# Two preactivated 5x5 self-correlation layers on one core: where the next unit's group average stands in TensorE's order

## What is computed

```python
norm = jnp.sqrt(jnp.sum(feature * feature, axis=1, keepdims=True))
fn = feature / jnp.maximum(norm, EPS)
fp = jnp.pad(fn, ((0, 0), (0, 0), (PAD, PAD), (PAD, PAD)))
corr = jnp.stack([jnp.sum(fp[:, :, r:h + r, cc:w + cc] * fn, axis=1)
                  for cc in range(K) for r in range(K)], axis=1)
cat = jnp.concatenate([feature, corr], axis=1)          # 512 + 25 channels
y = jnp.einsum('oc,bchw->bohw', conv_w, cat) + conv_b[None, :, None, None]
return jax.nn.relu(y)
```

## Time and profile before

| what | value |
|---|---|
| median of three runs | 527.68 us (525.36 to 530.27) |
| profiled execution, its own time | 526.55 us |
| span of the profiled execution | 524.8 us |
| TensorE busy | 470.0 us (90%) |
| VectorE busy | 370.0 us (71%) |
| ScalarE busy | 276.4 us (53%) |
| GpSimd busy | 127.6 us (24%) |
| mean granted TensorE clock | 0.967 of full speed |

### The profile page before, as it was taken

How to read it: one execution, slowest core, us unless ns; L and a number is a source line. 1 busy time by engine, 2 the same in 40 slices (tenths; PEclk the granted TensorE clock), 3 DMA queues, 4 the chain that set the end, 5 groups by cost and what they waited for, 6 DMA issues and landing times.

```text
span 524.8 us, 9885 instructions
## 1 busy us (share of the span) xinstructions
PE 470.0 (90%) x3880; PEld 259.5 (49%) x3880; DVE 370.0 (71%) x868; ACT 276.4 (53%) x370; POOL 127.6 (24%) x179
## 2 busy tenths in 40 slices
PE   0557597679996999999998999999999999999996
PEld 0443445364643646464553646464646455464442
DVE  4788896768967687786869495868878695623322
ACT  1443455447383665839383755657493848433222
POOL 3534420131330313131220313131312212140400
PEclk9978898879998999999999999999999999999999
DMA  8271263542220465447566673232322325463432
GB/s 297 108 252 51 87 201 117 138 117 54 82 82 8 118 213 164 128 158 242 203 213 223 208 267 117 55 115 55 86 85 50 114 72 176 146 189 106 148 115 107
DMA packets 50876, 71.76 MB, mean 137 GB/s; under 512 B 12276, under 2 KB 37932, under 8 KB 50830
## 3 DMA queue, kind: packets, MB, share of 16 engines
q1 hardware_dynamic: 41038, 62.21, 35.5%
q0 software_dynamic: 9792, 8.92, 7.1%
HBM read 34.97 MB, written 33.59 MB: 131 GB/s over the span
## 4 chain that ended last, share of the span: by engine, by line
PE 60%; DVE 18%; ACT 7%; DMA 6%; issue 4%; POOL 3%; SPq 1%; DVEq 0%; ACTq 0%; POOLq 0%
PE conv_ps L567 42%; PE gram_ps L487 8%; DVE operands L837 4%; DVE stats L790 4%; PE conv_ps L576 4%; DMA vol<-corr_h 4%; ACT operands L661 3%; ACT v L667 3%; PE gram_ps L499 2%; DVE xs L920 2%; POOL v L430 2%; DVE operands L843 1%; DMA xs<-in_x_dram 1%; PE turn_ps L557 1%; POOL vol L293 1%
## 5 line engine op out<-in xcount | busy, mean ns | idle before, releaser
L567 PE MATMUL conv_ps<-operands,wh 128*128 128x512 f16 x1024 | 326.0, 383 | 0.3 <-DVE wl L908 0.3
L567 PE MATMUL conv_ps<-operands,wl 128*128 128x512 f16 x512 | 195.8, 382 | 0.0
L694 ACT ACTIVATE act_out<-conv_ps,bias,wdown 128x512 f32<-128x512 f32 x128 | 95.9, 772 | 133.9 <-PE conv_ps L576 125.1
L567 PEld LDWEIGHTS conv_ps<-operands,wh 128*128 128x128 f16 x1024 | 100.8, 98 | 122.4 <-issue 4.8
L837 DVE TENSOR_TENSOR operands<-v,operands 128x1024 f16<-128x1024 f32 x64 | 81.5, 1274 | 59.1 <-ACT v L667 53.9
L920 DVE TENSOR_TENSOR xs<-xs,act_out 128x512 f32<-128x512 f32 x128 | 85.9, 683 | 36.6 <-ACT act_out L694 36.3
L790 DVE BATCH_NORM_STATS2 stats<-xs 128x6 f32<-128x512 f32 x128 | 79.7, 678 | 5.5 <-DMA xs<-in_x_dram 5.5
L661 ACT ACTIVATE operands<-xs,affine 128x1024 f16<-128x1024 f32 x64 | 78.5, 1233 | 5.6 <-DVE affine L830 5.6
L567 PEld LDWEIGHTS conv_ps<-operands,wl 128*128 128x128 f16 x512 | 50.5, 99 | 57.9 <-issue 1.5
L487 PE MATMUL gram_ps<-operands 128*64 128x192 f16 x960 | 74.3, 252 | 2.1 <-ACT band L675 2.1
L293 POOL DMA_DIRECT2D vol<-corr_h x48 | 35.5, 747 | 166.3 <-DVE corr_h L859 166.2
(11 more groups left out here) (80 smaller groups left out, 257.5 us busy)
## 6 DMA issues: line engine op xcount, KB each, us to landing
xs<-in_x_dram SPq DMA_DIRECT2D x32, 512.0 KB, 6.3
out_dram<-xs SPq DMA_DIRECT2D x32, 512.0 KB, 3.0
band_dram<-band SPq DMA_DIRECT2D x64, 192.0 KB, 3.2
skew<-band_dram SPq DMA_DIRECT2D x64, 133.0 KB, 3.0
vol<-corr_h POOLq DMA_DIRECT2D x48, 50.0 KB, 2.7
rows_dram<-rows SPq DMA_DIRECT2D x32, 65.8 KB
rows_dram<-rows SPq DMA_DIRECT2D x32, 63.3 KB
mirror<-rows_dram POOLq DMA_DIRECT2D x14, 110.9 KB, 2.5
```

The costliest lines, as they stand in the source:

```text
L567: pe.matmul(conv_ps[:, g % 4, :], w[:, l, t, m * P:(m + 1) * P], opnd[:, u % RING, part, t, n * HALF:(n + 1) * HALF], start=(t == 0 and w ...
L694: act.activation(act_out[:, g % 2, :], conv_ps[:, g % 4, :], ACT.Relu, bias=bias[:, l, m:m + 1], scale=wdown[:, l, m:m + 1]).then_inc(relu, 1)
```

## The change

The average of unit k + 1 is issued behind the fourth pair of products of slot k, where it stood between the second and the third. It concerns slots 3 to 14, twelve averages. The four averages of units 0 to 3 stay where they were.

```diff
                     for p in range(PAIRS):
                         products(k, p)
-                        if p == 1 and valid(k + 1):
-                            average(k + 1)
+                    if valid(k + 1):
+                        average(k + 1)
                 for j in range(GROUPS):
```

## The result

Twenty runs of each kernel: 528.26 us before (525.36 to 532.81), 531.9 us after (527.87 to 536.57), ratio 1.0059 with a 95% interval of 1.0032 to 1.0087. The change costs about 3 us; I had forecast 538.0 us, 10 to 11 us of loss. The profiled execution after took 531.42 us, its span is 529.7 us where it was 524.8.

What follows compares the result with a forecast made beforehand. TensorE, busy 90% of the span, was taken as the bound. 6.4 + 2.1 + 2.4 = 10.9 us on the profiled 526.55 us gave 537.5, set half a microsecond higher at 538.0 us; range 531.5 to 544.

Steps and rivals of the forecast that it cites:

- The chain: Steady slots, average to volume matmul: average issued 2.33 us later, normalisation, correlation and transfers into vol 1.9 us later.
- Slots 3 and 4: Normalisation 2.1 us late in slot 3, arriving undiminished at L547's wait in slot 4: cost 2.1 us (1.5 to 2.4).
- Quiet slots: Slots 3, 6 and 10 to 14, no image load in flight: no cost, and the average's own cost unchanged at 0.32 us.
- The margins: Quiet slots: the third transfer's lead over the volume matmul falls from 2.4 to 0.5 us, so no wait on vol.
- Crowded slots: Slots 5, 7, 8 and 9, image load in flight: wait on vol grows 1.6 us each, 6.4 us (5.6 to 7.6).
- The clock: Longer waits in slots 8 and 9 drop TensorE's clock: one and a half slow stretches, 2.4 us (0 to 3.3).
- Rival 3: Slots 7 to 9: transfer into vol lands in 2.7 us once the image load has drained; 525.4 us, chance 0.06.
- rival 2: Quiet slots' margins fail: landings up to 1 us longer in six slots add 6 us; 544 us, chance 0.11.
- rival 1: TensorE's clock stays up in slots 8 and 9: sum 8.5 us, 535.5 us, chance 0.20.

Runs made afterwards that it cites:

- the two reordered kernels: VectorE's correlation moved ahead of the next unit's low tiles, in the kernel before (522.66 us, ratio 0.9872) and in the changed kernel (521.64 us, ratio 0.9862).
- the run with the extra matmul at the end: The kernel before with one more fp32 matmul of the average's size behind the fourth pair in slots 3 to 14: ratio 1.0037.

## Why the prediction was wrong

In parts: 10.9 us were summed up, 6.4 for the waits on vol, 2.1 for slots 3 and 4, 2.4 for the clock and nothing for the average's own cost. The measured loss is 3.1 us.

- **The chain was right.** Average, scale, line 655 ahead of the band's copies, normalisation, correlation, transfer: each moved the way it was described. The sizes were a little less (the pairs take 2.13 us and not 2.33, because the 0.32 us between the average and the next product was not all that it cost in the middle; so the normalisation is 1.65 us late and not 1.9).
- **Slots 3 and 4: right.** Forecast 2.1 us; the profile means differ by 2.1 us (single profiles scatter by 5.4 and 3.6 us), and the kernel that is late there only loses 2.7 us (0.8 to 4.5). L547's wait was forecast at 6.5 us and is 6.1 to 6.6 us. The cause is VectorE's list with hardly a gap from the late normalisation to the weight remainders: L547 starts 46.7 us behind the normalisation in both profiles. That the first profiles differ by 2.9 us and not 2.1 goes with the lower clock in slot 3 after.
- **Quiet slots: the first step that failed.** "Its own cost is unchanged ... I count nothing for it", with a saving of 0.3 us x 12 named as a bound and put aside because "neither has a reason in a row". The trace of the kernel before had one, slot 15. Measured 0.29 us per slot, 2.9 us over slots 5 to 14 where no wait swallows it (the two reordered kernels show it in all ten), near the bound itself. The margins held, as forecast: no wait on vol in slots 10 to 14.
- **Crowded slots: the second, and the largest.** "So the delay goes straight into TensorE's wait", 4 x 1.6 us. The transfer's landing goes with the image load, which I had as the lower bound, but I moved the load by the 1.4 us of the last band copy. In the first pair of profiles it moved by between -1.1 and +2.3 us. It stands in SyncE's queue behind stores and the band's own landing; which of them moved it was not taken apart. On average the landing did not move at all (22.9 us into the slot). Slots 7 to 9 lose 0.3 us net by the profile means, some 1.2 us before the saving of 0.9; timed alone they lose 2.4 us (0.5 to 4.4), or 1.0 by the means of all runs. Slot 5, forecast at +1.6, had no wait in the first profile and 0.75 us in the second, and 1.18 us in the one that is late in slots 3 and 4 only, where its own average is in the middle.
- **The clock: the third.** 2.4 us were counted for the change. A stretch at half clock follows slot 7's wait after, but the kernel before loses two in its second profile, after 2.0 and 2.1 us of idleness. It is a cost of waiting in these slots in both kernels and cancels for the most part: over slots 7 to 9 the five profiles with the average in the middle have mean clocks of 1.00, 0.96, 1.00, 0.98 and 0.98, the four with it at the end 0.98 each, which is 1.4 and 1.7 us of lost clock per execution (already in the lengths above). That the rows before show 1.00 after a wait of 1.88 us was one draw.
- **Rival 3** (the transfer leaves the crowd) held in half: the crowded transfer shrank from 7.1 to 4.1 us in slot 8 and from 6.3 to 5.2 in slot 9. In slot 7 it grew from 5.3 to 6.0. I gave it 0.06 because I required it to shrink to 2.7.
- **Two sums of the rivals were off.** In rival 2 a landing 1 us later costs only what exceeds the margin of 0.5 us, so six slots would pay 3 us and not 6. Rival 3's 525.4 us lacks the half microsecond that the forecast and rival 1 have. Neither bears on the result.

What stays open: the profile means add up to 2.1 + 0.3 - 7 x 0.29 = 0.4 us, plus slot 5's tenths, while the timed ratios give 3.1 and 2.5 us, with intervals that reach down to 1.7 and 0.7. So 2 us or so of the measured loss are placed in no slot. Nine profiles that scatter by 4 us in slots 7 to 9 don't settle whether the late average costs 0.3 or 2.4 us there.

## What to carry over

When an instruction moves, price it in both places from a stretch of the same kernel that has none: here slot 15 against slot 12 would have shown 0.52 us for the average in the middle, where I had 0.32 in either place. When a wait ends with a transfer that shares the DMA engines with a large one, ask when the large one ends, since the small one's own issue time may count for little. And the head of a needless chain is better cut than moved: the correlation did not need the next unit's tiles, and putting it ahead of them gave 1.3%, twice what the average's place costs.

## What the runs showed of the hardware

- A 128x8 fp32 matmul between products that use 64 columns of the array costs 0.44 to 0.52 us, and 0.23 to 0.24 us where the 128-column convolution matmuls follow it. Why it is dearer in the middle was not tried.
- With the lists in their original order a transfer of 50 KB takes 2.3 to 3.1 us in slots without an image load and up to 8.7 us beside a load of 2 MB (slot 8 of the run with the extra matmul at the end). In slots 7 to 9 of the four profiles of the two kernels it landed 10.4 to 11.6 us after the load's issue, though its own issue moved by 1.65 us; the other profiles with full loads in their place widen this to 9.8 to 12.1 us. Issued ahead of the load, by the reordered correlation, the third transfer landed 4.3 to 8.1 us after the load's issue. The Trainium skill ("DMA: Bandwidth & Descriptors", Queues, rings and completion order) says that a DMA engine alternates between its queues packet by packet; this case does not show the small transfer getting through early: in slot 8 of the kernel before none of its packets starts within 4.4 us of the issue, and it lands 0.5 us behind its last packet. Whether its packets stood ready for the engines in that time is not in the trace.
- Of the waits on vol in slots 7 to 9 of nine profiles, those of 1.88 us and less left TensorE's granted clock at 1.00, four of the eight between 1.94 and 2.12 us were followed by a stretch at 0.50, and so were all four from 2.33 to 3.02 us. The kernel before shows both: 1.00 behind a wait of 1.88 us, 4 us at 0.57 behind waits of 2.00 and 2.09 us.
